# Half of a rank-256 product made transposed for pairs of tiles, and the seven products of a pair placed in one row

## What is computed

```python
logits = x @ Wr.T + 5.0 * one_hot(language_ids)      # 8 experts
gates  = softmax over the top 2 of logits            # 0 elsewhere
h      = einsum('btd,erd->bter', x, A)               # 8 x 16
c      = x @ W.T + 2.0 * einsum('bter,bte,eor->bto', h, gates, B)
out    = x + c @ (U * S @ V.T).T
```

## Time and profile before

| | us |
|---|---|
| median of 3 runs (lowest to highest) | 156.6 (156.23 to 157.12) |
| profiled execution | 156.3 |
| its span on the core | 154.5 |
| TensorE busy | 150.1 (97%) |
| VectorE, ScalarE, GpSimd busy | 102.7, 65.6, 69.9 |

### The profile page before, as it was taken

The page is one execution under the profiler, slowest core; times in us unless marked ns, Lnnn a source line. Parts: engine busy times, 40 slices in busy tenths (PEclk is TensorE's granted clock), DMA queues, the critical chain, the costliest instruction groups (busy, mean ns, idle before and its releaser), DMA issues.

```text
span 154.5 us, 2555 instructions
## 1 busy us (share of the span) xinstructions
PE 150.1 (97%) x883; PEld 139.9 (91%) x883; DVE 102.7 (66%) x299; ACT 65.6 (42%) x147; POOL 69.9 (45%) x53
## 2 busy tenths in 40 slices
PE   7999999999999999999999999999999999999991
PEld 5899999999988999989998999899999989998880
DVE  0887882942757898684669386929692967386862
ACT  4867772639615532551165125414431642233200
POOL 2000500259556650359355926591669068701800
PEclk9999999999999999999999999999999999999999
DMA  5999999994312064346338645764680087006184
GB/s 176 387 405 406 398 414 408 407 407 154 127 39 97 20 256 136 128 140 275 140 135 305 241 136 208 236 239 136 271 258 18 0 296 249 2 22 251 70 329 148
DMA packets 10669, 32.72 MB, mean 212 GB/s; under 512 B 1440, under 2 KB 1952, under 8 KB 10528
## 3 DMA queue, kind: packets, MB, share of 16 engines
q1 hardware_dynamic: 10368, 31.96, 55.7%
q10 hardware_dynamic: 288, 0.59, 1.0%
HBM read 24.16 MB, written 8.39 MB: 211 GB/s over the span
## 4 chain that ended last, share of the span: by engine, by line
PE 94%; DMA 3%; DVE 1%; ACT 0%; SPq 0%; issue 0%; DVEq 0%
PE pj L322 16%; PE pj L324 16%; PE pj L323 16%; PE fin L322 14%; PE fin L324 13%; PE fin L323 13%; DMA w_raw<-in_W 3%; PE zt L392 2%; PE gt L374 1%; PE zt L322 1%; PE zt L324 1%; PE zt L323 1%; DVE w_lo L704 0%; ACT w_hi L561 0%; DVE x_all L833 0%; SPq L217 0%
## 5 line engine op out<-in xcount | busy, mean ns | idle before, releaser
L278 POOL TENSOR_TENSOR xT_lo<-xt_raw,xT_hi 128x1024 fp32r<-128x1024 f32 x16 | 40.3, 2520 | 54.9 <-ACT xT_hi L576 54.9
L322 PE MATMUL pj<-proj_hi,xT_hi 128*128 128x392 f32 x128 | 45.0, 352 | 0.0
L324 PE MATMUL pj<-proj_hi,xT_lo 128*128 128x392 f32 x128 | 43.6, 341 | 0.0
L323 PE MATMUL pj<-proj_lo,xT_hi 128*128 128x392 f32 x128 | 43.5, 340 | 0.0
L293 POOL TENSOR_TENSOR x_all<-x_all,vw_raw 128x512 f32<-128x512 f32 x18 | 23.0, 1294 | 17.6 <-DVE vw_raw L808 17.6
L322 PE MATMUL fin<-v_hi,w_hi 128*128 128x256 f32 (+1 forms) x84 | 26.9, 320 | 0.1
L324 PE MATMUL fin<-v_hi,w_lo 128*128 128x256 f32 (+1 forms) x84 | 26.4, 314 | 0.0
L323 PE MATMUL fin<-v_lo,w_hi 128*128 128x256 f32 (+1 forms) x84 | 26.4, 314 | 0.0
L322 PEld LDWEIGHTS pj<-proj_hi,xT_hi 128*128 128x128 f32 x128 | 24.1, 188 | 1.0
L323 PEld LDWEIGHTS pj<-proj_lo,xT_hi 128*128 128x128 f32 x128 | 24.1, 188 | 0.5
L324 PEld LDWEIGHTS pj<-proj_hi,xT_lo 128*128 128x128 f32 x128 | 24.0, 188 | 0.0
(11 more groups left out here) (87 smaller groups left out, 230.6 us busy)
## 6 DMA issues: line engine op xcount, KB each, us to landing
xt_raw<-in_xt SPq DMA_DIRECT2D x16, 512.0 KB, 4.0
x_all<-in_x SPq DMA_DIRECT2D x16, 512.0 KB, 5.2
out<-x_all SPq DMA_DIRECT2D x13, 512.0 KB, 3.1
vw_raw<-in_VW SPq DMA_DIRECT2D x6, 384.0 KB, 6.7
w_raw<-in_W SPq DMA_DIRECT2D x8, 256.0 KB, 5.8
out<-x_all SPq DMA_DIRECT2D x5, 256.0 KB, 2.1
u_raw<-in_U SPq DMA_DIRECT2D x1, 1024.0 KB, 14.1
aw_raw<-in_AW SPq DMA_DIRECT2D x1, 544.0 KB, 6.8
```

Of the source, the lines that this page charges most:

```text
L278: nc.gpsimd.tensor_sub(xT_lo[:, t % 2, :, :], xt_raw[:, t % XTR, :, :], xT_hi[:, t % 2, :, :].bitcast(F32)).then_inc(xt_lo, 1)
L322: nc.tensor.matmul(dst, l_hi, r_hi, start=first, stop=False, skip_group_check=shared)
L323: nc.tensor.matmul(dst, l_hi, r_lo, start=False, stop=False, skip_group_check=shared)
L324: return nc.tensor.matmul(dst, l_lo, r_hi, start=False, stop=last, skip_group_check=shared)
```

## The change

Of the 392 columns of the projection, the last 128 (half of P, so half of z) are no longer made with the tokens in rows. TensorE's `project` makes 264 columns a tile, and `half_t(p)` makes the other half of z already transposed for both tiles of a pair: `proj` as weights, x^T of the two tiles as 256 streamed columns, 8 triples, into bank `zt`. Only the first half of z is copied and transposed, one transpose a tile, inside `half_t`. The mix writes into `zt` as well: two triples of 256 columns a pair in place of one of 256 a tile. gh of both tiles is transposed together, and split in one operation of 256 columns.

The order is by pairs now: two projections, then all seven products of the pair before, then the gh transposes, `half_t` and the mix. Pair 6, the last with seven products, has p4 and p3 behind the last mix; pairs 0 and 7 keep the plain form. The x^T parts have four buffers each instead of two, and to make room `b_raw` and `u_raw` lie in `w_raw`, so that their loads wait for counts of w_lo. The other engines' lists follow.

```diff
+    TCOLS = ER + E + P
-        xT_hi = sb("xT_hi", [P, 2, DC, P], F32R)
+        xT_hi = sb("xT_hi", [P, XTR, DC, P], F32R)
...
@@ sync
                 if k == 6:
-                    sp.dma_start(b_raw[:, :, :], B).then_inc(b_load, 16)
-            load_xt(1)
+                    sp.wait_ge(w_lo_done, 4)
+                    sp.dma_start(b_raw, B).then_inc(b_load, 16)
+            for t in range(1, XTR):
+                load_xt(t)
             sp.dma_start(s_col[:, :], S).then_inc(s_load, 16)
-            sp.dma_start(u_raw[:, :, :], U).then_inc(u_load, 16)
...
+            sp.wait_ge(w_lo_done, 12)
+            sp.dma_start(u_raw, U).then_inc(u_load, 16)
...
@@ gpsimd
+            pool.wait_ge(gh_done, 2)
+            split_x(3)
             pool.wait_ge(y_done, 2)
-            make_tsum(0)
-            make_tsum(1)
-            split_x(3)
-            pool.wait_ge(gh_done, 3)
-            make_tsum(2)
-            make_tsum(3)
...
+            for j in range(4):
+                make_tsum(j)
+            for p in range(1, PAIRS):
+                if p < PAIRS - 1:
+                    pool.wait_ge(gh_done, 2 * p + 2)
+                    split_x(2 * p + 2)
+                    split_x(2 * p + 3)
+                if p >= 2:
+                    pool.wait_ge(fin_read, READS * (p - 2) + 1)
+                    side(2 * p - 1, 0, 1)
+                    side(2 * p - 2, 1, 1)
+                    pool.wait_ge(fin_read, READS * (p - 2) + 3)
+                    side(2 * p - 1, 1, 2)
@@ tensor
+            def half_t(p):
+                r = (2 * p) % XTR
+                dst = zt_v[:, 1, :, :]
+                for k in range(DC):
+                    last = triple(dst, proj_hi[:, k, TCOLS:COLS], proj_lo[:, k, TCOLS:COLS],
+                                  xT_hi[:, r:r + 2, k, :], xT_lo[:, r:r + 2, k, :], k == 0, False, shared=True)
+                    if k == 2:
+                        pe.wait_ge(z_copied, 2 * p + 2)
+                        for t in range(2):
+                            nc.tensor.matmul(zt_v[:, 0, t, :], z_sb[:, t, :], ident[:, :], start=False, stop=False,
+                                             is_transpose=True, skip_group_check=True)
+                last.then_inc(xt_used, 1)
...
-            step(0)
-            step(1, mix_at=5)
-            step(2, gh_at=5, mix_at=DC - 1, z_later=True)
-            for s in range(3, TILES):
-                step(s)
+            project(0)
+            make_bv()
+            project(1)
+            half_t(0)
+            transpose_gh(0)
+            for p in range(1, PAIRS):
+                project(2 * p)
+                project(2 * p + 1)
+                if p == 1:
+                    pe.wait_ge(us_lo_done, MC)
+                    pe.wait_ge(za_lo, 1)
+                    expand(0, bank_a, 0, 0, BANK)
...
+                else:
+                    first_part(p - 1)
+                    if p < PAIRS - 1:
+                        second_part(p - 1)
+                transpose_gh(p)
+                zt_free(p)
+                half_t(p)
+                mix(p)
...
@@ vector
+            def pair(p):
+                split_za(p - 1)
+                if p == 1:
+                    split_zb_plain(0)
+                    split_us(0)
+                    split_us(1)
+                else:
+                    sums(p - 1)
+                    split_zb(p - 1)
+                gates_top(2 * p)
+                gates_apply(2 * p)
+                gates_top(2 * p + 1)
+                gates_apply(2 * p + 1)
+                if p == 1:
+                    residual_end(0, bank_a, 0, 0, BANK)
+                    residual_end(1, bank_b, 0, BANK, D)
+                    split_t(0)
+                    residual_end(2, bank_c, 1, 0, BANK)
+                    residual_end(3, bank_d, 1, BANK, D)
+                    split_gh(p)
+                    split_t(1)
                 else:
+                    up(p - 1, 1)
+                    up(p - 1, 2)
+                    xb1(p - 1)
+                    xa0(p - 1)
+                    split_gh(p)
```

More of the change, by code:

```diff
@@ L365, in p_chunk @@
                     last.then_inc(w_used, 1)
[L367 to L374, removed]
-            def mix(t):
-                pe.wait_ge(gt_lo, t + 1)
-                triple(pj[t % 2][:, Z0:COLS], ghT_hi[:, :], ghT_lo[:, :], bv_hi[:, :], bv_lo[:, :],
-                       False, True, shared=True).then_inc(z_done, 1)
@@ L381, in transpose_z, with project @@
-            def transpose_z(t):
-                p = t // 2
-                pe.wait_ge(z_copied, t + 1)
-                if p >= 1 and t % 2 == 0:
+            def project(t):
+                q, r = t % 2, t % XTR
+                pe.wait_ge(xt_lo, t + 1)
+                if t >= 2:
+                    pe.wait_ge(gh_done, t - 1)
+                    pe.wait_ge(z_copied, t - 1)
+                for k in range(DC):
+                    if t == 0 and k == 0:
+                        pe.wait_ge(aw_lo, 1)
+                    if t == 0 and k % 2 == 0:
+                        pe.wait_ge(p_lo, k // 2 + 1)
+                    last = triple(pj[q][:, 0:TCOLS], xT_hi[:, r, k, :], xT_lo[:, r, k, :],
+                                  proj_hi[:, k, 0:TCOLS], proj_lo[:, k, 0:TCOLS], k == 0, k == DC - 1)
+                    if t == 2 and k == MH:
+                        mix(0)
+                last.then_inc(pj_done, 1)
@@ L389, in transpose_z, with transpose_gh, mix @@
                     pe.wait_ge(sums_done, 4 * (p - 1))
-                c = RANK * (t % 2)
+            def transpose_gh(p):
+                pe.wait_ge(gh_done, 2 * p + 2)
+                if p >= 1:
+                    pe.wait_ge(gt_lo, p)
+                for t in range(2):
+                    last = nc.tensor.transpose(gt[:, t * P:(t + 1) * P], gh[:, t, :], ident[:, :])
+                last.then_inc(gt_done, 1)
+            def mix(p):
+                if p == 0:
+                    pe.wait_ge(bv_lo_done, 1)
+                pe.wait_ge(gt_lo, p + 1)
                 for m in range(MC):
-                    last = nc.tensor.transpose(zt[:, c + m * P:c + (m + 1) * P], z_sb[:, m * P:(m + 1) * P], ident[:, :])
+                    cols = slice(m * P, (m + 1) * P)
+                    last = triple(zt[:, 2 * m * P:2 * (m + 1) * P], bv_hi[:, cols], bv_lo[:, cols],
+                                  ghT_hi[:, :], ghT_lo[:, :], False, True, shared=True)
                 last.then_inc(zt_done, 1)
@@ L690, in _ @@
             split_us(1)
-            for s in range(1, TILES):
-                step(s)
-            split_gh(LAST)
-            copy_z(LAST)
+            for p in range(1, PAIRS):
+                pair(p)
+            split_za(PAIRS - 1)
             split_zb_plain(PAIRS - 1)
```

279 lines of the change are left out of this document (98 added, 181 removed).

## The result

The changed kernel takes 160.28 us (median of four runs, 160.14 to 160.61) against 156.86 for the kernel before on the same chip (four runs, 156.23 to 157.44): a ratio of 1.022, with a 95% interval from 1.018 to 1.027. It is slower, by 2.2%. 161.3 was forecast, with 157.7 to 163.0 as range. The profiled execution took 160.16, its span is 158.4 (before 154.5), so 3.9 us are to be explained (by the medians 3.4; 4.7 were forecast).

A forecast was written before the change was run, and what follows sets the result against it. TensorE's issue time was taken as the bound. 0.2 issue + 1.45 products + 2.0 start + 1.35 mix(1) - 0.27 old wait = +4.7 us, 161.3 us on the median, range 157.7 to 163.0.

The forecast's parts named there:

- Step 1: TensorE's issue: cheaper projections and two fewer z transposes against 24 more half_t matmuls, +0.03 us a pair, +0.2 in all.
- Rival E: Projection and half_t: matmuls of the new shapes start with less fixed cost, so not slower, 156.6 or below; chance 0.12.
- Step 2: Seven products in a row: p4 right behind p2 waits for the second up addition, 0.29 us in five pairs, 1.45.
- T + 3.54 against T + 3.69: In step 2, from the start of the second projection's last matmul: TensorE through p2, against the second up addition's end.
- Step 3: The start: project(0) at 28.15 as before; TensorE waits for both us_lo before pair 0's expansion, 2.0 us with restart.
- B: At the start, VectorE keeps the port for both us_lo, wait 0.7 instead of 2.0 us: 160.0 us; chance 0.27.
- D: GpSimd keeps the port: all tsum before us_lo, the next xT_lo before the T split: 164.5 us; chance 0.08.
- C: The start is covered, us_lo and T split not held, only the products wait: 158.0 us; chance 0.13.
- Step 4: Mix(1): TensorE waits for ghT_lo, behind a T split held by GpSimd's xT_lo, 1.35 us with restart.
- Step 5: The tail: same set of matmuls, p4 and p3 behind mix(7) cover the z split; nothing gained or lost.
- The clock: Left out of the sum: a waiting TensorE also lowering its clock, since no wait is above 2 us.

The follow-up runs named there:

- e6: Changed kernel with projections of eight widths by tile, 264 to 384 columns, the extra columns unused, to measure matmul spacing: one execution, 169.44 us.
- e1: Changed kernel with ScalarE's split of x^T of tile 1 moved back behind the four splits of P: 159.8 us, ratio 1.022.
- e3: Changed kernel with GpSimd waiting for the gating of tile 2 between its second and third tsum: 159.46 us, ratio 1.021.
- e4: Changed kernel with VectorE's first T split moved from between pair 0's residuals to behind ghT_lo of pair 1: 160.09 us, ratio 1.024.
- e2: Changed kernel with a pair's two gh transposes moved from behind p3 to between p2 and p4: 159.8 us, ratio 1.020.
- e5: Changed kernel with e1, e2, us_lo ahead of tile 1's gating, T splits ahead of xT_lo, GpSimd not waiting for a gating: 159.03 us, ratio 1.014.
- e7: e5 with GpSimd waiting for gating of tiles 0 and 1 before xT_lo of tile 3, second us_lo behind tile 1's gating, other moves: 155.89 us, ratio 0.997.
- e8: e7 with all of half_t between p2 and p4, and pair 0's z transposes behind the seventh triple: 154.65 us, ratio 0.988.

## Why the prediction was right, and where not

**Step 1, the issue, was mis-sized.** The term was +0.2 and measured -1.3 us. The step that failed is the price of the two new widths: "`half_t` is priced as the 256 row, 0.120", a row of P, and 0.124 for 264 on a line that begins at that row. half_t's matmuls stand at 0.118 and 264 columns at 0.121 (e6). 48 x 0.003 + 24 x 0.002 = 0.19 a pair, 1.5 us in all. The line held; its end, taken from another stage of the kernel, did not. Rival E had the mechanism right and its sign; it needed 8.2 ns a matmul to cancel the waits, and 2 to 3 were there. By the formula of the Trainium skill, "TensorE: Matmul & The Clock Gate", section "Back-to-back issue gap", the prediction had worked out, as an estimate, -0.17 a pair, and -0.16 was measured. That is luck. The page gives the formula for a matmul by itself and not for a stream, and its spacing isn't met: 0.1125 for 264 columns by the formula, 0.121 by the trace. In the trace 24 more starts cost 0.27 a pair, and 0.18 of it come back since a matmul of 264 columns costs less beyond its columns than one of 392; with the 0.23 of two z transposes that makes -0.14.

**Step 2, p4, was right**: 1.45 forecast, 1.49 measured, with the second `up` addition as releaser. The slack of T + 3.54 against T + 3.69 could be read from rows of another place because both sides were counted from the same matmul.

**Step 3, the us_lo, was right; the start was not.** TensorE's wait was forecast as 2.0 with restart and measured 2.09. Both ends of that wait came some 0.8 later than forecast, through the later start. The two us_lo took 4.11 and the four tsum 7.12, 2.0 longer than alone, as when the two engines take turns one by one. Rivals B and D, in which one engine keeps the port, fall, and so does C, in which nothing waits; by its time alone B, with 160.0, was nearer to the 160.28 than the forecast. The Trainium skill, "SBUF — State Buffer", section "Who interferes with whom", says of the shared pair that the one that issues first has it for the whole instruction; the trace agrees, and shows besides that they take turns when both are waiting.

But the step also said "project(0) begins at 28.15, as before", and it began at 29.25. Two things were left out. ScalarE's split of tile 1 now stands ahead of the last part of W; it waited for x^T (0.53, at 23.27), and w_hi came behind it. And GpSimd's xT_lo of tile 1 then met the last w_lo, which took 2.49 instead of 0.69. b_lo, behind it in VectorE's queue, pushed proj_lo to 28.43, which is the second gap. The step asked whether the moved loads would be late, not what the instructions of the moved split would hold. e1 shows that this one place is worth the whole 1.1 us of the profiled execution. Three smaller slips changed nothing: the loads did not all have 10 us to spare (ScalarE waited 1.00 for B, before the change 0.83); the 42.91 holds five eighths of project(2), not five sixths; and by its own terms the issue of a pair is 14.74, not 14.75, and the end of the gating in step 2 is T + 2.3, not T + 2.4.

**Step 4, mix(1), had the mechanism right and the size too large**, 0.92 for 1.35. The split of T was held as forecast (2.45). TensorE was ready at 58.65 instead of 57.8, 0.85 later, since the us_lo that it had waited for ended at 49.72 instead of 48.85. ghT_lo ended at 59.42 instead of 59.0, only 0.42 later. What was mis-sized is the chain from us_lo to ghT_lo: from the end of dtop of tile 2 (50.90) to the next exponential (53.17) ScalarE took 2.27, where 2.6 were forecast, and the rest of the chain was 0.1 shorter too. e3 and e4 show how the waits hang together: what is taken from one of them comes back for 0.7 of 1.1 at mix(1), or for nearly all at the next p4, where VectorE is no earlier.

**Step 5, the tail**, brought nothing, as forecast.

**The clock.** "That a waiting TensorE also lowers its clock I leave out: no wait is above 2 us" left out something that happens. In the traces of e2 and e5 the granted clock falls to the 1.2 GHz level behind the long wait at the start (1.96 and 2.63 us). The mean clock is 0.985 to 0.989 in 12 of the 22 executions of the five kernels with such a wait, the changed kernel's among them, in none of the 16 of e3, e7 and e8, and in one of the 37 of the kernel before beside the experiments (another stood at 0.661). For the executions without a trace it isn't shown where the clock fell. It costs 1.6 us on the spot in e2; between executions of one kernel the low clock made from 0.1 (the changed kernel) over 0.7 to 0.9 (e1, e4, e2) to 1.9 (e5). That it made less than 1.6 can come from the later waits, which a later TensorE finds shorter: in e2 the one at mix(1) is gone.

So the forecast came within 1 us by misses that nearly cancel: the missed start, +1.1, against the issue, 1.5 too high, and mix(1), 0.4 too high. That the time fell so near to the forecast is in part luck. What was right without luck is p4 and the us_lo, 3.6 of the 5.6 us of waits, and that TensorE's waits decide.

## What to carry to other kernels

When TensorE issues without gaps, count what a change makes it issue, from rows of the same widths if any exist, but spend the most care on the first pass through the new order: there queues of other engines are written anew, and here 4.1 of 5.6 us were lost in them. Of every instruction that moves to another place, on any engine, ask which later instruction of that engine it now precedes, what it waits for itself, and which VectorE operation takes turns with it if it is GpSimd's. A price read from rows of another stage is an estimate even at the same width. A wait that seems to slow GpSimd may be what keeps the port clear for a chain of small operations; take it away only together with a look at what those do then.

## What was not expected of the hardware

- A matmul's cost beyond its columns at 2.4 GHz is not fixed: in the projections 11 ns at 264 columns, 12 to 13 from 272 to 304, 15 at 384 (e6). Matmuls of 256 columns stood at 0.120 in P and at 0.118 in half_t; why they differ isn't settled.
- Behind a single wait of TensorE of 1.96 us (e2) the granted clock fell to the 1.2 GHz level from 50.50 to 53.91; behind one of 1.98, in the profiled execution of the changed kernel, it stayed at 1.00. What decides it wasn't found.
- An operation on eight columns can take 2.2 us: `gate`, with both inputs in SBUF, waited for an xT_lo of GpSimd (2.21 in e5, 2.28 in e7, 0.17 when GpSimd rests).
